# Transposing the normalised rows of the next batch by block transposes and SBUF transfers instead of by TensorE, with the adapter's steps at earlier slots

## The reference

```
x += layernorm(x + relu(x@W1[l] + b1[l])@W2[l] + b2[l]) * gamma[l] + beta[l]     # L0, hidden width 64
x += x @ weight[s].T + bias[s]                                                # L1, 256 x 256
x += gated sum of five relu networks 256 -> 1024 -> 256                       # L2, by far the most work
x += prefix / suffix / all-but-self attention pooling of x                    # L3
```

## Time and profile before

| | |
|---|---|
| median of 3 runs | 506.36 us (505.79 to 509.01) |
| profiled execution, its own time | 505.66 us |
| its span in the profile | 503.3 us |
| PE busy | 495.1 us, 98% |
| DVE busy | 348.8 us, 69% |
| ACT busy | 261.1 us, 52% |
| POOL busy | 235.1 us, 47% |
| granted TensorE clock | 1.0 of full speed throughout |
| chain that ended last | PE 91%, DVE 7%, ACT 1% |

### The profile page before, as it was taken

How to read it: one execution, slowest core, us unless ns; L and a number is a source line. 1 busy time by engine, 2 the same in 40 slices (tenths; PEclk the granted TensorE clock), 3 DMA queues, 4 the chain that set the end, 5 groups by cost and what they waited for, 6 DMA issues and landing times.

```text
span 503.3 us, 7021 instructions
## 1 busy us (share of the span) xinstructions
PE 495.1 (98%) x2335; PEld 408.9 (81%) x2335; DVE 348.8 (69%) x701; ACT 261.1 (52%) x507; POOL 235.1 (47%) x201
## 2 busy tenths in 40 slices
PE   8999999999999999999999999999999999999996
PEld 5788888888888878888888887888888888888984
DVE  5587226874687798785578689688468779735277
ACT  4655654443556574535356665444355657445234
POOL 1584455445355445444644436444535544655022
PEclk9999999999999999999999999999999999999999
DMA  5956354222264442422237453422222342430002
GB/s 157 195 170 149 113 156 138 84 85 84 85 140 129 113 111 84 130 82 91 75 101 186 97 174 104 126 84 85 84 84 85 104 106 83 123 129 3 1 0 83
DMA packets 77657, 52.97 MB, mean 105 GB/s; under 512 B 40758, under 2 KB 67382, under 8 KB 77622
## 3 DMA queue, kind: packets, MB, share of 16 engines
q1 hardware_dynamic: 75734, 50.44, 34.9%
q10 hardware_dynamic: 1888, 2.10, 1.3%
HBM read 48.33 MB, written 2.10 MB: 100 GB/s over the span
## 4 chain that ended last, share of the span: by engine, by line
PE 91%; DVE 7%; ACT 1%; issue 0%; POOL 0%; DVEq 0%; ACTq 0%; POOLq 0%
PE ps_hid L841 14%; PE ps_hid L842 14%; PE ps_hid L846 14%; PE ps_net L898 13%; PE ps_net L903 13%; PE ps_net L899 13%; PE ps_net L870 2%; DVE hid_lo L1815 1%; DVE prob L1467 1%; PE ps_net L663 1%; PE ps_side L534 1%; PE ps_side L538 1%; PE ps_side L533 1%; PE ps_side L547 1%; PE ps_side L544 1%; PE ps_hid L684 1%
## 5 line engine op out<-in xcount | busy, mean ns | idle before, releaser
L1907 POOL TENSOR_TENSOR wi_lo<-raw_wi,wi_hi 128x512 fp32r<-128x512 f32 x78 | 103.2, 1323 | 211.4 <-ACT wo_hi L1091 113.6
L1112 ACT ACTIVATE hid_hi<-ps_hid 128x512 fp32r<-128x512 f32 x160 | 95.7, 599 | 196.7 <-PE ps_hid L846 195.0
L1815 DVE SCALAR_TENSOR_TENSOR hid_lo<-ps_hid,hid_hi 128x512 fp32r<-128x512 f32 x160 | 110.2, 689 | 118.8 <-ACT hid_hi L1112 117.6
L841 PE MATMUL ps_hid<-x2T_hi,wi_lo 128*128 128x512 f32 (+1 forms) x332 | 125.8, 381 | 0.0
L842 PE MATMUL ps_hid<-x2T_hi,wi_hi 128*128 128x512 f32 (+1 forms) x332 | 125.2, 379 | 0.0
L898 PE MATMUL ps_net<-hid_hi,wo_hi 128*128 128x512 f32 x304 | 118.8, 391 | 0.0
L899 PE MATMUL ps_net<-hid_hi,wo_lo 128*128 128x512 f32 x304 | 118.5, 390 | 0.0
L1908 POOL TENSOR_TENSOR wo_lo<-raw_wo,wo_hi 128x512 fp32r<-128x512 f32 x78 | 104.3, 1337 | 0.0
L846 PE MATMUL ps_hid<-x2T_lo,wi_hi 128*128 128x512 f32 (+1 forms) x332 | 98.9, 379 | 0.0
L903 PE MATMUL ps_net<-hid_lo,wo_hi 128*128 128x512 f32 x304 | 93.8, 390 | 0.0
L842 PEld LDWEIGHTS ps_hid<-x2T_hi,wi_hi 128*128 128x128 f32 x332 | 62.5, 188 | 11.7
(11 more groups left out here) (329 smaller groups left out, 502.3 us busy)
## 6 DMA issues: line engine op xcount, KB each, us to landing
raw_wi<-in_L_cond_share_wi_dram SPq DMA_DIRECT2D x23, 512.0 KB, 3.7
raw_wo<-in_L_cond_share_wo_dram SPq DMA_DIRECT2D x23, 512.0 KB, 4.8
raw_wi<-in_L_cond_expert_wi_dram SPq DMA_DIRECT2D x16, 512.0 KB, 3.7
raw_wo<-in_L_cond_expert_wo_dram SPq DMA_DIRECT2D x16, 512.0 KB, 4.8
next_x2T<-in_x_dram SPq DMA_DIRECT2D x24, 64.0 KB, 4.3
x_rows<-in_x_dram SPq DMA_DIRECT2D x3, 512.0 KB, 3.7
x_rows<-netT SPq DMA_DIRECT2D x48, 32.0 KB, 2.0
out_dram<-out_rows SPq DMA_DIRECT2D x5, 256.0 KB, 5.6
```

What stands on the lines that cost most here:

```text
L841: mm(dst, wi_lo[:, w, k, c], x2T_hi[:, k, rows], start=(k == 0), stop=False)
L1112: fn(hid_hi[:, ring(b, q)], ps_hid[:, ring(b, q)], ACT.Relu).then_inc(hid_hi_ready, 1)
L1815: v.scalar_tensor_tensor(out=hid_lo[:, ring(b, q)], in0=ps_hid[:, ring(b, q)], scalar=0.0, in1=f32(hid_hi[:, ring(b, q)]), op0=ALU.max, op ...
L1907: g.tensor_tensor(wi_lo[:, w], raw_wi[:, half % 2, :, c], f32(wi_hi[:, w]), ALU.subtract)
```

## The change

`stage_a` gets a new table of slots, new steps, and other places to keep intermediate results. The eight PE transposes of a batch's normalised rows go. In their place DVE turns 32x32 blocks of `norm` (two STREAM_TRANSPOSE of 128x512) into `x_rows` under the name `norm_blocks`, and 16 transfers from SBUF to SBUF put the blocks in their places in `next_x2T` under the name `normT`: 12 issued by SP, 4 by ACT. DVE then computes both `x1T` from SBUF in slot 34. Two of the four normalisations go to ACT, with a small DVE instruction (`neg_shift`) ahead of them. The turned L1 weights are kept in `prob` instead of `norm`.

```diff
-    A_SLOT = dict(w1=20, blocks=20, xT=22, w2=25, subj_blocks=25, hid=26, subj_w=27, adapt=28, stats=29, xb=31, norm=30, normT=32, x1_hi=33, x1_lo=35, y=36, base=37)
-    GATE_SUM = {23: 0, 27: 1, 38: 2}
+    A_SLOT = dict(w1=18, blocks=18, xT=20, w2=20, hid=24, subj_blocks=25, subj_w=26, adapt=26, stats=27, norm=28, xb=29, place=30, x1T=34, x1_hi=34, x1_lo=35, y=36, base=37)
+    GATE_SUM = {23: 0, 30: 1, 38: 2}
...
+        def place_norm(queue, a, columns):
+            for c in columns:
+                src = norm_blocks[a * BK:(a + 1) * BK].rearrange("p (n s) -> p n s", s=P)[:, :, c * BK:(c + 1) * BK]
+                dst = normT[c * BK:(c + 1) * BK].rearrange("p (n s) -> p n s", s=P)[:, :, a * BK:(a + 1) * BK]
+                queue.dma_start(dst, src).then_inc(norm_in, 16)
...  (SP, at the end of a batch's loads)
+                if not last:
+                    sp.wait_ge(a_dve.sem, a_dve.at(b + 1, "norm_blocks"))
+                    for a in range(P // BK - 1):
+                        place_norm(sp, a, range(P // BK))
...  (PE)
-            def normalised(slot, i):
-                if 0 <= slot - A_SLOT["normT"] < KD:
-                    k = slot - A_SLOT["normT"]
-                    pe.wait_ge(a_dve.sem, a_dve.at(i, "norm"))
-                    for r in range(R):
-                        last = nc.tensor.transpose(ps_side[:, k, r * P:(r + 1) * P], norm[:, r, k * P:(k + 1) * P], ident[:])
-                    last.then_inc(a_pe.sem, 1)
...  (ACT)
+                if slot == A_SLOT["norm"]:
+                    act.wait_ge(a_dve.sem, a_dve.at(i, "shift"))
+                    for r in range(R // 2):
+                        last = fn(norm[:, r], norm[:, r], ACT.Identity, bias=neg_shift[:, r:r + 1], scale=rstd[:, r:r + 1])
+                    last.then_inc(a_act.sem, 1)
+                if 0 <= slot - A_SLOT["place"] < 2:
+                    if slot == A_SLOT["place"]:
+                        act.wait_ge(a_dve.sem, a_dve.at(i, "norm_blocks"))
+                    first_c = (slot - A_SLOT["place"]) * 2
+                    place_norm(act, P // BK - 1, range(first_c, first_c + 2))
...  (DVE)
-                    for r in range(R):
+                    v.scalar_tensor_tensor(out=neg_shift[:], in0=mean[:], scalar=-1.0, in1=rstd[:], op0=ALU.mult, op1=ALU.mult).then_inc(a_dve.sem, 1)
+                    for r in range(R // 2, R):
                         last = v.tensor_scalar(norm[:, r], norm[:, r], mean[:, r:r + 1], rstd[:, r:r + 1], ALU.subtract, ALU.mult)
                     last.then_inc(a_dve.sem, 1)
-                if 0 <= slot - A_SLOT["normT"] < KD:
...
+                    dve.wait_ge(a_act.sem, a_act.at(i, "norm"))
+                    for k in range(KD):
+                        blocks = norm_blocks.rearrange("p (k r s) -> p k r s", k=KD, s=P)[:, k]
+                        last = v.transpose(blocks, norm[:, :, k * P:(k + 1) * P])
+                    last.then_inc(a_dve.sem, 1)
+                if slot == A_SLOT["x1T"]:
+                    dve.wait_ge(norm_in, 16 * (P // BK) ** 2 * i)
+                    here("xb1")
+                    for k in range(KD):
+                        v.scalar_tensor_tensor(out=x1T[:, k], in0=normT[:, k * S:(k + 1) * S], scalar=gamma[:, k:k + 1], in1=xbT[:, k],
+                                               op0=ALU.mult, op1=ALU.add).then_inc(a_dve.sem, 1)
```

More of the change, by code:

```diff
@@ L246, in cond_resid_program @@
         x_blocks, xT = next_x2T, x1T
-        subj_blocks, subj_wT = subj_w, norm[:, 0:KD]
+        subj_blocks, subj_wT = subj_w, prob[:, 0].rearrange("p (k d) -> p k d", d=D)
+        norm_blocks, normT = x_rows[:].rearrange("p r d -> p (r d)"), next_x2T[:].rearrange("p k s -> p (k s)")
         row_blocks = netT[:, NG - 1].rearrange("p k s -> p (k s)")
@@ L257, in cond_resid_program @@
         x0_in = [sem("x0_in0"), sem("x0_in1")]
-        blocks_in, rows_in, x_in, subj_in, subj_b_in, out_stored = sem("blocks_in"), sem("rows_in"), sem("x_in"), sem("subj_in"), sem("subj_b_in"), sem("out_stored")
+        blocks_in, rows_in, norm_in, x_in, subj_in, subj_b_in, out_stored = sem("blocks_in"), sem("rows_in"), sem("norm_in"), sem("x_in"), sem("subj_in"), sem("subj_b_in"), sem("out_stored")
         w1_in, b1_in, b2_in, w2_in, beta_in, gamma_in = sem("w1_in"), sem("b1_in"), sem("b2_in"), sem("w2_in"), sem("beta_in"), sem("gamma_in")
@@ L273, in cond_resid_program @@
         evac_dve = Steps(sem("evac_dve"), "g0 g1 g2 g3")
[L275 to L278, removed]
+        a_pe = Steps(sem("a_pe"), "hid adapt0 adapt1 y0 y1", 1)
+        a_act = Steps(sem("a_act"), "xhi0 xhi1 hid_below hid_up subj_w_hi norm x1hi0 x1hi1", 1)
+        a_dve = Steps(sem("a_dve"), "w1_hi xT0 xT1 xlo0 w2_hi w2_up b2_hi b2_lo xlo1 hid_sum hid_hi hid_lo subj_wT subj_w_lo sum0 sum1 stats sums mean var_eps "
+                                    "shift norm norm_blocks xb0 xb1 x1T0 x1T1 x1lo0 x1lo1 x2T0 x2T1", 1)
         a_pool = Steps(sem("a_pool"), "w1_lo w2_lo rstd", 1)
@@ L916, in batch @@
                         second_product(b, s, first, last)
-                    if not last:
-                        normalised(q, b + 1)
                     if not first:
@@ L1268, in stage_a @@
                     dve.wait_ge(a_pool.sem, a_pool.at(i, "rstd"))
-                    for r in range(R):
+                    v.scalar_tensor_tensor(out=neg_shift[:], in0=mean[:], scalar=-1.0, in1=rstd[:], op0=ALU.mult, op1=ALU.mult).then_inc(a_dve.sem, 1)
+                    for r in range(R // 2, R):
                         last = v.tensor_scalar(norm[:, r], norm[:, r], mean[:, r:r + 1], rstd[:, r:r + 1], ALU.subtract, ALU.mult)
                     last.then_inc(a_dve.sem, 1)
-                if 0 <= slot - A_SLOT["normT"] < KD:
[L1273 to L1277, removed]
+                    here("norm")
+                    dve.wait_ge(a_act.sem, a_act.at(i, "norm"))
[9 more added lines that the diff above has]
+                                               op0=ALU.mult, op1=ALU.add).then_inc(a_dve.sem, 1)
                 if slot == A_SLOT["x1_lo"]:
```

## The result

The changed kernel takes **524.6 us** (median of 4 runs, 523.37 to 527.51), the kernel before 507.69 (4 runs, 505.79 to 509.4): a ratio of **1.036 [1.034, 1.039]**. The forecast was 519 us and the range ended at 525. The ratios compare the undisturbed executions of both kernels and are not the quotient of the medians. The profiled execution took 524.69 us, its span is 522.9 us; before, the span was 503.3, so 19.6 us are to be explained.

The account below looks back on a forecast made before the run. PE, busy 98% of the span, was taken to bound the kernel. To the profiled 505.66 us came -2.8 + 10.2 + 4.8 + 0.9 = +13.1, giving 518.8, forecast as 519 us; range 511 to 525.

Parts of the forecast that it names:

- Transposes, -2.8: Six groups of four transposes leave PE's list in batches 0 to 2, 0.46 us each: -2.8 us.
- The adapter's slot, +10.2: PE waits for `subj_w_lo` before the second half of `adapt`, 3.4 us in each of three batches: +10.2 us.
- Slots 18 to 22, +4.8: In batches 1 and 2, DVE's added steps delay `pooled`, through `tsum_lo` and the output rows, 2.4 us each: +4.8 us.
- y, +0.9: Later `x1hi` and slower `x1T` beside POOL's split cost 0.3 us in each of three batches before `y`: +0.9 us.
- What is hidden: Normalisations on ACT, `neg_shift`, block transposes and transfers finish before DVE's reader in slot 34, with 2.4 us of room.
- The rival of late blocks: Blocks land late for DVE in slot 34 and PE waits before `y`: 522 to 528 us; chance 13%.
- The clock: Rival: after the 3.4 us stall a slot passes at half clock, 2.7 us more per batch: 527 us; chance 8%.
- the main case: The summed terms, with PE waiting at the adapter and at `pooled` and a clock of 1.0 throughout: 519 us; chance 70%.

Follow-up runs that it names:

- the filled wait: The changed kernel with twelve 128x512 matmuls of zeros on PE ahead of the kept wait for `subj_w_lo` at the adapter: 520.17 us, ratio 1.0281.

## Why the prediction was wrong

The direction and the places were right, the size was 5.6 us short. That the median still lies inside the range, by 0.4 us, is luck: this end was set for blocks that land late, and none did. The steps that failed are the clock, put at nothing in the sum, and the lateness before `tsum`. By its own steps:

- **Transposes, -2.8.** Right in size: 3.0 us of loop, by the slots and between two kernels that differ by the way of the rows and little else.
- **The adapter's slot, +10.2.** Right: 10.2, by the mechanism forecast (the slot itself gave back 0.11 each time, which the sum had not). `subj_wT_lo` took 1.33 against the 1.35 forecast and ended 0.55 us behind POOL's instruction, as the row of L1226 had it. Removing the wait, and only that, removed the delay. The Trainium skill's rule (SBUF — State Buffer, "Who interferes with whom"), weighed in the prediction, agrees here too: beside POOL 1.33, ahead of it 0.67, without it 0.69.
- **Slots 18 to 22, +4.8.** Too small: 2.9 + 3.6 = 6.5. The step that failed is "PE is late by as much", 0.76 us for the copy and the transpose. The wait for `tsum` grew by 1.45. I moved the list by 0.76 but took the duration of the subtraction L1548 as it was (0.68), though it stands between them and `tsum`, and the move brought it beside POOL's split: 1.42, 0.74 more. My upper end of 6.5 had this contention, but only for the subtraction behind `tsum` and W2's copies. The second wait, 1.8 for 1.65 forecast, is about right.
- **y, +0.9.** Nothing in the length of the slots; the weight loads show three waits of 0.2. `x1T` did take longer (2.44 us for two in batch 1) and was covered by the room.
- **What is hidden.** Right: SP's twelve issues took 8.12 us, forecast 8.3, the blocks landed in 1.9 to 2.1, and DVE did not wait for `norm_in`. The rival of late blocks did not come. But the room was smaller than the 2.4 us forecast: in batch 1 the last issue ended at 243.29 and DVE's reader began at 246.49, which with 2.0 for the landing leaves about 1.2. A part of it went to `neg_shift`, which the working had at nothing. It stood beside POOL and took 1.25 us.
- **The clock.** This is the larger error. "A clock of 1.0 throughout" is wrong, and so is how I set the chances. I held the clock for a rival of the main case, at 8%, when it can only stand on top of the wait that the main case itself forecasts. Given a wait of 3.4 us, it fell after all three in the changed kernel, after two of three with the transposes on PE, and after two of three with the early steps two slots later. Its price was also too high. I took a whole slot at half speed, 2.7 us, and the windows, the slots and the filled wait show 1.6 to 1.7. The page of the Trainium skill on TensorE: Matmul & The Clock Gate, "What's actually happening", which was cited there (an idle PE goes to half rate), is borne out by this trace in its direction, 0.50 in the window from 222 to 224 us; the waits of 3.4 us with no fall behind them show that it does not follow each time. I let the clean clock of before speak against it, though that kernel had no such wait.

With the measured terms the sum is 505.66 - 3.0 + 10.2 - 0.3 + 6.4 + 5.0 = 524.0. To this come 1.4 us of the opening, and 0.6 go, because the time around the span is 1.8 us in this profiled execution and was 2.4 in the one before: 524.8, against 524.69 measured.

**What stays open.** What decides whether the clock falls after a wait was not settled, for 1.9 us or for 3.4. Why the opening took 21.2 us in one profiled execution and 23.3 in another was not settled either; it makes differences of span below some 2 us uncertain, and the lengths of the slots are the better measure.

## What to carry to other kernels

When a producer is moved into the slot of its reader, write out all that the producing engines have ahead of it there and which of it meets GpSimd, and ask whether the reader needs the wait there at all: here it did not, and dropping one line gave back 15.2 us of the loop. A wait of TensorE of some 3 us may cost its length and half as much again through the clock behind it. Compare two traces by their slots, too: an account that meets the whole span can do so by an error that the opening covers. Moving a list by a fraction of a microsecond can carry a later subtraction of two SBUF inputs into GpSimd's time and double it, so look at each instruction between the moved one and its reader.

## What the runs showed of the hardware

- The slow clock comes after the wait. PE resumed at 94.25 us after 3.4 us of waiting, and its matmuls had their full pitch until 95.3 to 95.6; the slow stretch lasted to about 99.2.
- The same wait of 3.4 us was followed by it three times of three in one kernel, two of three in two others. A wait of 2.4 us was followed by it once. Waits of 1.9 us: two of three in the profiled execution. Waits of 1.5: none of three.
- Twelve matmuls in each wait kept it away: the adapter's slot took 7.18 us all three times, and the mean clock was 0.996 to 0.999 in the four executions, no lower than in the kernel without the wait (0.995 to 1.0).
- A 32-partition subtraction is held up by GpSimd as much as one of 128 partitions: 1.42 for 0.68. Even `neg_shift`, of 128x4 elements, took 1.25 us: from 230.85 to 232.10, beside a POOL instruction from 230.78 to 232.07. An instruction of the same kind and size took 0.15 with no POOL beside it (at 229.28).
- Where DVE's subtraction began 0.32 us ahead of POOL's it took its 0.68; POOL's lasted 1.52, against 1.29 in the earlier trace rows.
